# Keys and values as plain float32 products beside a split query product, in a cross-attention kernel on one core

## What is computed

```python
q = (layernorm(x) @ Wq + bq)          # 16 heads of 16
k, v = split(ctx @ Wkv + bkv)
attn = softmax(q @ k.T / 4)           # per head, 128 x 128
x1 = x + (attn @ v) @ Wo + bo
n = layernorm(x1)
scores = n @ w_router                 # the best 96 tokens of 128 are chosen
y = n, with the chosen rows replaced by gelu(n @ w_block)
out = x1 + y
```

## Time and profile before

| | before |
|---|---|
| median of 3 runs | 956.26 us (955.37 to 956.96) |
| the profiled execution, its own time | 957.89 us |
| its span | 956.0 us |
| granted TensorE clock, mean | 0.985 of full speed |
| TensorE products busy | 892.5 us, 93% |
| TensorE weight loads busy | 757.0 us, 79% |
| VectorE busy | 849.6 us, 89% |
| ScalarE busy | 894.6 us, 94% |
| GpSimd busy | 814.4 us, 85% |

### The profile page before, as it was taken

The page is one execution under the profiler, slowest core; times in us unless marked ns, Lnnn a source line. Parts: engine busy times, 40 slices in busy tenths (PEclk is TensorE's granted clock), DMA queues, the critical chain, the costliest instruction groups (busy, mean ns, idle before and its releaser), DMA issues.

```text
span 956.0 us, 33133 instructions
## 1 busy us (share of the span) xinstructions
PE 892.5 (93%) x10276; PEld 757.0 (79%) x10276; DVE 849.6 (89%) x2568; ACT 894.6 (94%) x4612; POOL 814.4 (85%) x1514
## 2 busy tenths in 40 slices
PE   3699999999999999999999999999999999999870
PEld 2578888888888888888888888888888888888750
DVE  5688899999999999999999999999999999998754
ACT  2699999999999999999999999999999999999950
POOL 5257878999999999999999999999999999988777
PEclk9999999999999999999999999999999999999995
DMA  5222212322232232223223222322222232221102
GB/s 155 76 63 64 68 45 71 89 66 75 85 86 60 82 88 70 72 84 91 56 83 88 71 72 84 90 56 83 87 70 73 83 91 57 82 66 46 35 23 77
DMA packets 71245, 70.84 MB, mean 74 GB/s; under 512 B 12192, under 2 KB 62880, under 8 KB 71072
## 3 DMA queue, kind: packets, MB, share of 16 engines
q1 hardware_dynamic: 71072, 68.73, 25.2%
HBM read 35.13 MB, written 16.78 MB: 54 GB/s over the span
## 4 chain that ended last, share of the span: by engine, by line
PE 88%; ACT 5%; issue 2%; POOL 2%; DVE 1%; SPq 1%; DMA 1%; POOLq 0%; ACTq 0%; DVEq 0%
PE ps_q L272 18%; PE ps_s L306 14%; PE ps_a L355 13%; PE ps_a L279 12%; PE ps_t L279 11%; PE ps_a L272 9%; PE ps_t L327 8%; ACT e_sb L477 4%; PE ps_q L342 3%; DMA x_sb<-in_x 1%; POOL x_sb L834 1%; SPq L234 0%; POOL z_sb L817 0%; DVE neg_max L551 0%; PE ps_t L441 0%
## 5 line engine op out<-in xcount | busy, mean ns | idle before, releaser
L477 ACT ACTIVATE e_sb<-ps_s,neg_max 128x128 f32<-128x128 f32 x2048 | 724.9, 459 | 1.2 <-DVE neg_max L551 1.0
L477 ACT ACTIVATION_READ_ACCUMULATOR e_sb<-ps_s,neg_max 128x1 f32 x2048 | 588.3, 299 | 0.0
L551 DVE TENSOR_REDUCE neg_max<-ps_s 128x4 f32<-128x512 f32 x512 | 332.0, 669 | 64.4 <-PE ps_s L306 62.2
L306 PE MATMUL ps_s<-q_eo,k_sb 32*128 32x256 f32 x2048 | 146.8, 399 | 15.9 <-ACT e_sb L477 6.4
L768 POOL TENSOR_TENSOR v_pad<-v_sb,recip 128x256 f32<-128x256 f32 x128 | 79.6, 622 | 78.1 <-DVE recip L589 78.0
L355 PE MATMUL ps_a<-e_sb,v_pad 128*32 128x128 f32 x4096 | 138.4, 276 | 0.7 <-DVE x_sb L559 0.6
L279 PE MATMUL ps_a<-w_o_sb,o_sb 128*128 128x256 f32 x512 | 135.9, 388 | 2.9 <-DVE v_sb L635 2.4
L279 PE MATMUL ps_t<-w_z_sb,xt_sb 128*128 128x258 f32 x512 | 133.4, 383 | 2.9 <-DVE z_sb L646 2.9
L306 PEld LDWEIGHTS ps_s<-q_eo,k_sb 32*128 32x128 f32 x2048 | 95.8, 184 | 45.4 <-issue 42.4
L355 PEld LDWEIGHTS ps_a<-e_sb,v_pad 128*32 128x32 f32 x4096 | 104.1, 109 | 22.4 <-issue 21.2
L758 POOL TENSOR_TENSOR x_sb<-x_sb,bo_sb 128x256 f32<-128x256 f32 x128 | 121.3, 947 | 0.2
(11 more groups left out here) (80 smaller groups left out, 2249.2 us busy)
## 6 DMA issues: line engine op xcount, KB each, us to landing
x_sb<-in_x SPq DMA_DIRECT2D x64, 256.0 KB, 2.9
c_sb<-in_ctx SPq DMA_DIRECT2D x64, 256.0 KB, 3.1
q_eo<-q_raw SPq DMA_DIRECT2D x512, 32.0 KB, 2.0
out<-z_sb SPq DMA_DIRECT2D x64, 256.0 KB, 2.4
z_sb<-in_L_xattn_Wkv SPq DMA_DIRECT2D x2, 256.0 KB, 5.1
z_sb<-in_L_xattn_Wq SPq DMA_DIRECT2D x1, 256.0 KB, 2.9
w_o_sb<-in_L_xattn_Wo SPq DMA_DIRECT2D x1, 256.0 KB, 6.5
w_z_sb<-in_L_ffn_w_block SPq DMA_DIRECT2D x1, 256.0 KB, 5.5
```

Of the source, the lines that this page charges most:

```text
L306: mm = nc.tensor.matmul(ps_s[:, bank(b, j), c, :, :], k_sb[rows, r2, c, h * T:(h + 1) * T], q_eo[rows, r2, :, c, h, :], start=True, stop=True)
L477: last = nc.scalar.activation(e_sb[:, b % 4, j, c, par, :], ps_s[:, bank(b, j), c, par, :], ACT.Exp, bias=neg_max[:, b % 4, h:h + 1], accu ...
L551: nc.vector.tensor_reduce(neg_max[:, b % 4, :].rearrange("p (c j q) -> p j c q", c=C, j=J)[:, j, :, :], ps_s[:, bank(b, j), :, :, :], AX.X ...
```

## The change

Keys and values are made with `full_terms` from float32 operands. Only the queries keep `three_terms`. So only x is split: `x_hi` by ScalarE and `x_lo` by VectorE, each of 128 x 256 elements. ScalarE copies the transposed ctx to `c_t` as float32, as a second instruction. `inputs_low` waits for this second copy, which stands behind the first on the same engine. TensorE waits for `c_t_ready` beside `t_lo_ready` wherever it writes `ps_t` again, and before the keys. The weights `w_k_sb` and `w_v_sb` are loaded directly and not split.

```diff
             def values(b):
-                    pe.wait_ge(w_lo_ready["v"], 1)
+                    pe.wait_ge(w_in["v"], 16)
...
-                three_terms(ps_v,
-                            lambda a, c: (t_hi, t_lo)[a][:, n, 1, c, h * T:(h + 1) * T],
-                            lambda a, c: (w_hi, w_lo)[a]["v"][:, c, :]).then_inc(v_mm, 1)
+                full_terms(ps_v,
+                           lambda c: c_t[:, n, c, h * T:(h + 1) * T],
+                           lambda c: w_v_sb[:, c, :]).then_inc(v_mm, 1)
...
             def block_product(b):
                 pe.wait_ge(t_lo_ready, upto(b + 9))
+                pe.wait_ge(c_t_ready, upto(b + 9))
...
             def queries_or_keys(b, kind):
                 for m in range(C):
-                    mm = three_terms(ps_q[:, m * 2 * T:(m + 1) * 2 * T],
-                                     lambda a, c: (w_hi, w_lo)[a][w][:, c, m * P:(m + 1) * P],
-                                     lambda a, c: (t_hi, t_lo)[a][:, (b // 2) % 4, kind, c, :])
+                    if kind == 0:
+                        mm = three_terms(ps_q[:, m * 2 * T:(m + 1) * 2 * T],
+                                         lambda a, c: (w_q_hi, w_q_lo)[a][:, c, m * P:(m + 1) * P],
+                                         lambda a, c: (x_hi, x_lo)[a][:, (b // 2) % 4, c, :])
+                    else:
+                        mm = full_terms(ps_q[:, m * 2 * T:(m + 1) * 2 * T],
+                                        lambda c: w_k_sb[:, c, m * P:(m + 1) * P],
+                                        lambda c: c_t[:, (b // 2) % 4, c, :])
...
             def inputs_high(b):
-                    nc.scalar.copy(t_hi[:, n, :, :, h * T:(h + 1) * T].rearrange("p k c t -> p (k c) t"),
-                                   ps_t[:, :].rearrange("p (n t) -> p n t", t=T)).then_inc(t_hi_ready, 1)
+                    nc.scalar.copy(x_hi[:, n, :, h * T:(h + 1) * T],
+                                   ps_t[:, 0:E].rearrange("p (n t) -> p n t", t=T)).then_inc(t_hi_ready, 1)
+                    nc.scalar.copy(c_t[:, n, :, h * T:(h + 1) * T],
+                                   ps_t[:, E:2 * E].rearrange("p (n t) -> p n t", t=T)).then_inc(c_t_ready, 1)
...
             def inputs_low(b):
-                    dve.wait_ge(t_hi_ready, upto(b))
-                    part = (slice(None), n, slice(None), slice(None), slice(h * T, (h + 1) * T))
-                    nc.vector.tensor_tensor(t_lo[part].rearrange("p k c t -> p (k c) t"),
-                                            ps_t[:, :].rearrange("p (n t) -> p n t", t=T),
-                                            t_hi[part].rearrange("p k c t -> p (k c) t").bitcast(f32),
+                    dve.wait_ge(c_t_ready, upto(b))
+                    nc.vector.tensor_tensor(x_lo[:, n, :, h * T:(h + 1) * T],
+                                            ps_t[:, 0:E].rearrange("p (n t) -> p n t", t=T),
+                                            x_hi[:, n, :, h * T:(h + 1) * T].bitcast(f32),
                                             ALU.subtract).then_inc(t_lo_ready, 1)
...
             def weights_high(s):
-                for n, first in WEIGHTS:
-                    if s == first:
-                        act.wait_ge(w_in[n], 16)
-                        nc.scalar.activation(w_hi[n][:, :, :], raw_w[n], ACT.Copy,
-                                             scale=SCALE if n == "q" else 1.0).then_inc(w_hi_ready[n], 1)
+                if s == -5:
+                    act.wait_ge(w_in["q"], 16)
+                    nc.scalar.activation(w_q_hi[:, :, :], raw_w_q, ACT.Copy, scale=SCALE).then_inc(w_q_hi_ready, 1)
```

More of the change, by code:

```diff
@@ L57, in cross_attention_routed_ffn @@
         xhat = sb("xhat", [P, 4, E])
-        t_hi = sb("t_hi", [P, 4, 2, C, 2 * T], f32r)
-        t_lo = sb("t_lo", [P, 4, 2, C, 2 * T], f32r)
+        x_hi = sb("x_hi", [P, 4, C, 2 * T], f32r)
+        x_lo = sb("x_lo", [P, 4, C, 2 * T], f32r)
+        c_t = sb("c_t", [P, 4, C, 2 * T])
         q_raw = sb("q_raw", [P, 2, C, 2, T])
@@ L71, in cross_attention_routed_ffn @@
         g_sb = sb("g_sb", [P, 4, E])
-        w_hi = {n: sb(f"w_{n}_hi", [P, C, E], f32r) for n in "qkv"}
-        w_lo = {n: sb(f"w_{n}_lo", [P, C, E], f32r) for n in "qkv"}
+        w_q_hi = sb("w_q_hi", [P, C, E], f32r)
+        w_q_lo = sb("w_q_lo", [P, C, E], f32r)
+        w_k_sb = sb("w_k_sb", [P, C, E])
+        w_v_sb = sb("w_v_sb", [P, C, E])
         w_o_sb = sb("w_o_sb", [P, C, E])
@@ L105, in cross_attention_routed_ffn @@
         raw = z_sb[:, :, :].rearrange("p b e -> p (b e)")
[L106 to L109, removed]
+        raw_w_q = raw[:, 0:C * E].rearrange("p (c e) -> p c e", c=C)
         ps_s = ctx.enter_context(nc.psum_tensor("ps_s", [P, J + 1, C, 2, T], f32))
@@ L144, in cross_attention_routed_ffn @@
         bq_scaled = sem("bq_scaled")
-        w_hi_ready = {n: sem(f"w_{n}_hi_ready") for n in "qkv"}
-        w_lo_ready = {n: sem(f"w_{n}_lo_ready") for n in "qkv"}
+        w_q_hi_ready, w_q_lo_ready = sem("w_q_hi_ready"), sem("w_q_lo_ready")
         w_mean_mm, w_z_ready = sem("w_mean_mm"), sem("w_z_ready")
@@ L153, in cross_attention_routed_ffn @@
         t_hi_ready = sem("t_hi_ready")
-        t_lo_ready = sem("t_lo_ready")
+        t_lo_ready, c_t_ready = sem("t_lo_ready"), sem("c_t_ready")
         q_mm = sem("q_mm")
@@ L192, in cross_attention_routed_ffn @@
         block = ctx.enter_context(nc.Block())
-        WEIGHTS = (("q", -5), ("k", -4), ("v", -3))
         FIRST, LAST = -10, B + 17
@@ L236, in _ @@
             load_x(0)
-            sp.dma_start(raw_w["q"], w_q.rearrange("(c p) e -> p c e", p=P)).then_inc(w_in["q"], 16)
+            sp.dma_start(raw_w_q, w_q.rearrange("(c p) e -> p c e", p=P)).then_inc(w_in["q"], 16)
             load_c(0)
-            sp.dma_start(raw_w["k"], w_kv[:, 0:E].rearrange("(c p) e -> p c e", p=P)).then_inc(w_in["k"], 16)
+            sp.dma_start(w_k_sb[:, :, :], w_kv[:, 0:E].rearrange("(c p) e -> p c e", p=P)).then_inc(w_in["k"], 16)
             with nc.allow_non_contiguous_dma(reason="vectors of 256 elements, once"):
@@ L245, in _ @@
             load_x(2)
-            sp.dma_start(raw_w["v"], w_kv[:, E:2 * E].rearrange("(c p) e -> p c e", p=P)).then_inc(w_in["v"], 16)
+            sp.dma_start(w_v_sb[:, :, :], w_kv[:, E:2 * E].rearrange("(c p) e -> p c e", p=P)).then_inc(w_in["v"], 16)
             load_x(4)
@@ L321, in transpose_inputs @@
                     pe.wait_ge(t_lo_ready, upto(b - 1))
+                    pe.wait_ge(c_t_ready, upto(b - 1))
                 for kind in range(2):
@@ L393, in queries_or_keys @@
                     return
-                w = "qk"[kind]
                 if kind == 0:
@@ L401, in queries_or_keys @@
                 else:
-                    pe.wait_ge(t_lo_ready, upto(b + 1))
+                    pe.wait_ge(c_t_ready, upto(b + 1))
                     if has(b - 6):
@@ L407, in queries_or_keys @@
                 if b == 0:
-                    pe.wait_ge(w_lo_ready[w], 1)
+                    if kind == 0:
+                        pe.wait_ge(w_q_lo_ready, 1)
+                    else:
+                        pe.wait_ge(w_in["k"], 16)
                 for m in range(C):
-                    mm = three_terms(ps_q[:, m * 2 * T:(m + 1) * 2 * T],
-                                     lambda a, c: (w_hi, w_lo)[a][w][:, c, m * P:(m + 1) * P],
-                                     lambda a, c: (t_hi, t_lo)[a][:, (b // 2) % 4, kind, c, :])
+                    if kind == 0:
+                        mm = three_terms(ps_q[:, m * 2 * T:(m + 1) * 2 * T],
+                                         lambda a, c: (w_q_hi, w_q_lo)[a][:, c, m * P:(m + 1) * P],
+                                         lambda a, c: (x_hi, x_lo)[a][:, (b // 2) % 4, c, :])
+                    else:
+                        mm = full_terms(ps_q[:, m * 2 * T:(m + 1) * 2 * T],
+                                        lambda c: w_k_sb[:, c, m * P:(m + 1) * P],
+                                        lambda c: c_t[:, (b // 2) % 4, c, :])
                 mm.then_inc((q_mm, k_mm)[kind], 2)
@@ L431, in candidates @@
                     pe.wait_ge(t_lo_ready, upto(b + 17))
+                    pe.wait_ge(c_t_ready, upto(b + 17))
                     r = b % R
@@ L439, in keep_columns @@
                     pe.wait_ge(t_lo_ready, upto(b + 21))
+                    pe.wait_ge(c_t_ready, upto(b + 21))
                     pe.wait_ge(z_ready, upto(b + 11))
@@ L529, in weights_low @@
             def weights_low(s):
[L530 to L535, removed]
+                if s == -5:
+                    dve.wait_ge(w_q_hi_ready, 1)
+                    nc.vector.scalar_tensor_tensor(w_q_lo[:, :, :], raw_w_q, SCALE, w_q_hi[:, :, :].bitcast(f32),
+                                                   ALU.mult, ALU.subtract).then_inc(w_q_lo_ready, 1)
                 if s == 0:
@@ L644, in product_scaled @@
                     if b == 0:
-                        dve.wait_ge(w_lo_ready["v"], 1)
```

(1 more changed line is left out.)

## The result

The changed kernel takes 980.88 us (median of 4 runs, 980.09 to 981.5), beside 956.1 us for the kernel before, run beside it: 1.026 of it, with a 95% interval of 1.0247 to 1.0273. The forecast was 980 us, slower with a chance of 0.94.

The account below looks back on a forecast made before the run. TensorE was taken to bound the kernel, with ScalarE close behind. Added products of 36 us less 12 us of waits given back made 24 us on top of 956.26, so 980 us, with a range of 972 to 997.

Parts of the forecast that it names:

- The price of the products: On TensorE, float32 values and keys together add 0.30 us per step, 36.3 us over 121 steps.
- What is given back: TensorE's waits for ScalarE, 14.3 us over 121 steps, mostly vanish as its step grows; 12 us taken off.
- ScalarE's copy: On ScalarE, one copy of 512 becomes two of 256, 0.02 us more per step, hidden behind TensorE's longer step.
- No gain from `x_lo`: On VectorE, `inputs_low` falls by 0.27 us per step but brings nothing, as VectorE is not on the chain.
- late next: VectorE's residual waits for the projection, which ends about 0.45 us later in key steps; before, 2.9 us in 14 waits.
- Nothing given back: Rival: VectorE's wait for the projection delays ScalarE and the next scores, so TensorE's waits stay; 992 us, chance 0.17.
- ScalarE as the bound: Rival: the split copy costs a full 0.42 us per step on ScalarE; 989 or 1007 us, chance 0.08.
- Weight loads: Rival: loads of about 190 ns per product pace TensorE, so fewer products make it faster; 940 us, chance 0.04.
- Most absorbed: Rival: ScalarE is the real bound near 6.95 us a step and hides most of the 0.30; 956 to 970, chance 0.04.
- the ring: Last transposition, `inputs_high`, twelve exponentials, next scores: each waits on the one before; hardly longer or shorter than TensorE's own step.

## Why the prediction was right

*The price of the products.* Values 0.87 against 0.72 and keys 1.73 against 1.42 us are what the projection's rows gave: 0.15 and 0.155 us per step, 0.305 where 0.30 was taken. The same shape in the same kernel was the right place to look. The two products alone make 1.0242.

*What is given back.* I took 12 us. The chain says 1.1% of "issue" before and 0.0% after, and the sum agrees: 121 x 0.305 = 37 us of work, 24 us of time, 13 given back. The values alone show it most directly, with 5.4 us seen of 17.5 added.

The working of this term was luckier than its value. I called all of the 1.7% outside TensorE a wait. But ScalarE's 0.7% of the earlier trace rows is not spread over the steps: all of it lies behind 873.43 us, where the chain goes over to ScalarE at the end of the program.

```profile
873.43 3.65 ACT e_sb L477 x21
```

What I left out is that a wait also makes the scores' piece longer, 1.15 us in place of 1.08. The two errors nearly cancel. I also left 2 us of waits in the query steps for the wrong reason: with the products alone most of these steps are at 6.92, TensorE's own 6.78 and 0.15 for the values, and what is lost in the changed kernel is most likely the second copy's.

*ScalarE's copy.* This term was wrong in size. "0.02 us more" and "Nobody sees it" took 0.25 us for a copy of 256, the distance behind `xt_sb`; the distances of the new copies are 0.27 and 0.26. The pair costs 0.05 us, and in the kernel before it costs 6.8 us by itself, 0.056 per step. In the changed kernel it is covered in key steps by TensorE's longer step and is some 2 us in all. The estimate by the Trainium skill's "ScalarE: Activation LUTs", section "What ACT_TABLE_LOAD costs", was 0.092 us per step; the measured 0.056 lies between it and mine.

*VectorE.* No gain from `x_lo`: right, shown by 0.9991 in the run of its own. The residual's wait, named as late next, stayed small at 3.1 us.

*The rivals.* Nothing given back: refuted by the values alone, and by 25 us in place of 36. ScalarE as the bound: refuted by 196.77 of 200 us and by the copy in two, 7 us and not 33 to 51. Weight loads: refuted by 1.73 us for eight products with eight loads against 1.42 for twelve with twelve. Most absorbed: true of the values alone, not of both.

What the prediction lacked is the rule by step. It took averages over key and query steps. In the changed kernel each step is the longer of TensorE's own and the ring's: 7.22 us with keys and 6.97 with queries from start to start. The average came out right since the query step ended where the two meet. In the kernel before the rule holds for pairs of steps at best, as the 6.78 and 7.10 us show.

## What to carry to other kernels

Where two engines are both over 99% busy in the middle, neither busy share tells what an edit is worth: follow the chain of waits, compare a step with waits to one without, and price an operation by the same shape elsewhere in the same kernel. The first microseconds of added work go into the waits and cost little, the next cost their full price, and work removed from a step that is at the ring's floor gives nothing; so two edits that look small one by one can cost more together than their sum (13 and 5 us alone, 23 together). A split of one copy into two costs its full price where the engine's queue or a ring sets the step (6.8 us before the change) and a part of it where another engine sets most steps (some 2 us after it).

## What was not expected of the hardware

Three float32r products with 256 columns took 0.36 us and the one float32 call that replaces them 0.43 (half of 0.86), so the split form, with more loads and more instructions, is the faster one here as far as TensorE is concerned.

The order of shapes on TensorE has a price of its own. A full-array group behind the scores' products of 32 rows paid 0.19 us more than behind the transpositions (1.06 against 0.87), while the transpositions took 0.59 us in either place. The projection paid as much behind the small transposition of the kept rows (1.06 against 0.86). Why the transpositions of the inputs don't pay it was not tried.
